# A pre-LN LRU/attention/MoE kernel on one core: three shared batches ahead of the expert tiles, one batch's gathers moved into attention, and a start of attention on two queues

## What is computed

```python
x = x + lru_block(layernorm(x))                     # layer 0: linear recurrence and an MLP
x = x + moe0(layernorm(x))                          # 8 experts of hidden 256, top 2 by softmax
x = x + attention(layernorm(x), Wq, Wk, Wv, Wo)     # layer 1: causal, 16 heads of 8
x = x + moe1(layernorm(x))                          # 8 experts of hidden 512, top 2, and a shared expert

def moe1(x):                                        # cut
    up = einsum('th,ehi->tei', xf, up_w) + up_b
    eo = einsum('tei,eih->teh', gelu(up), down_w) + down_b
    combined = einsum('teh,te->th', eo * 0.1, w)    # w: gates of the top 2
    shared = (gelu(xf @ sw_up + sb_up) @ sw_down + sb_down) * 0.1
    out = shared + combined
    return out / (max(abs(out), -1) + 1e-06)
```

## Time and profile before

| | |
|---|---|
| median of 3 runs | 972.75 us |
| lowest and highest | 966.61, 973.84 us |
| profiled execution | 970.3 us |
| its span on the chip | 968.5 us |
| mean granted TensorE clock | 0.92 |
| PE busy | 808.7 us (83%) |
| DVE busy | 613.9 us (63%) |
| ACT busy | 521.3 us (54%) |
| POOL busy | 422.9 us (44%) |

### The profile page before, as it was taken

The page is one execution under the profiler, slowest core; times in us unless marked ns, Lnnn a source line. Parts: engine busy times, 40 slices in busy tenths (PEclk is TensorE's granted clock), DMA queues, the critical chain, the costliest instruction groups (busy, mean ns, idle before and its releaser), DMA issues. The chain is left out here.

```text
span 968.5 us, 18634 instructions
## 1 busy us (share of the span) xinstructions
PE 808.7 (83%) x5585; PEld 603.0 (62%) x5585; DVE 613.9 (63%) x1402; ACT 521.3 (54%) x1092; POOL 422.9 (44%) x524
## 2 busy tenths in 40 slices
PE   2798825898559899999999999986388899999993
PEld 2566615888425556565555565546256899999762
DVE  5478653557438977877777777733811665678457
ACT  3466466665315576767767666764131466565520
POOL 2655467727578013242333332224467700273174
PEclk9899866999759999999999999995589999999997
DMA  5930013555253121212131221000012322232222
GB/s 147 366 103 1 23 46 120 158 144 139 65 171 123 39 94 39 98 33 99 43 101 65 65 97 42 26 1 0 28 44 74 106 66 76 81 114 77 77 66 65
DMA packets 82157, 80.45 MB, mean 83 GB/s; under 512 B 9858, under 2 KB 61760, under 8 KB 82112
## 3 DMA queue, kind: packets, MB, share of 16 engines
q1 hardware_dynamic: 73122, 62.68, 20.9%
q0 software_dynamic: 8192, 16.79, 5.7%
q10 hardware_dynamic: 796, 0.42, 0.2%
HBM read 41.06 MB, written 38.80 MB: 82 GB/s over the span
## 5 line engine op out<-in xcount | busy, mean ns | idle before, releaser
L1661 ACT ACTIVATE Pb<-ps,low 128x512 f32<-128x512 f32 x320 | 216.7, 689 | 134.4 <-PE ps L1760 87.6
L931 POOL DMA_INDIRECT YG<-yslots,slot x128 | 132.1, 1032 | 152.1 <-DMA yslots<-yb 82.0
L1539 DVE TENSOR_REDUCE m<-ps 128x4 f32<-128x1024 f32 x128 | 156.2, 1221 | 55.1 <-PE ps L1737 36.0
L1760 PE MATMUL ps<-Q,KZ 128*128 128x128 f32 (+3 forms) x512 | 172.1, 397 | 5.0 <-ACT Pb L1661 4.0
L390 POOL DMA_INDIRECT xslots<-XN,slot x128 | 124.7, 974 | 69.9 <-issue 37.6
L1471 POOL TENSOR_SCALAR_AFFINE_SELECT Pb<-Pb 128x512 f32<-128x512 f32 (+1 forms) x84 | 67.7, 806 | 190.0 <-ACT Pb L1661 189.3
L1760 PEld LDWEIGHTS ps<-Q,KZ 128*128 128x128 f32 x512 | 93.0, 192 | 81.8 <-ACT Pb L1661 56.1
L1313 PE MATMUL ps<-xT,wst 128*128 128x128 f32 x960 | 136.5, 280 | 7.4 <-DVE wst L1182 4.6
L1325 PE MATMUL ps<-wst,hb 128*128 128x128 f32 x960 | 134.0, 276 | 6.6 <-ACT hb L1132 6.1
L1135 ACT ACTIVATE hb<-ps,upb 128x128 f32<-128x128 f32 x320 | 91.6, 369 | 75.0 <-PE ps L1313 74.9
L1313 PEld LDWEIGHTS ps<-xT,wst 128*128 128x128 f32 x960 | 122.6, 196 | 9.1 <-DVE wst L1182 5.8
(11 more groups left out here) (258 smaller groups left out, 1240.3 us busy)
## 6 DMA issues: line engine op xcount, KB each, us to landing
xt<-xslots SPq DMA_DIRECT2D x40, 256.0 KB
yslots<-yb SPq DMA_DIRECT2D x40, 256.0 KB, 2.3
terms<-high SPq DMA_DIRECT2D x32, 256.0 KB, 2.1
Q<-terms SPq DMA_DIRECT2D x128, 48.0 KB
KZ<-terms SPq DMA_DIRECT2D x128, 48.0 KB
xslots<-YG SPq DMA_DIRECT2D x2, 2560.0 KB, 11.8
terms<-low SPq DMA_DIRECT2D x16, 256.0 KB, 2.3
X<-in_L_attn_x_dram SPq DMA_DIRECT2D x4, 512.0 KB, 5.7
```

The source lines that it names most:

```text
L931: pool.indirect_dma_start(out=s.YG[:, TB * w + j, k, :], out_offset=None, in_=s.yslots[group][:, :], in_offset=bass.IndirectOffsetOnAxis(a ...
L1539: w = dve.tensor_reduce(top[:, :, (TB + 1, 3, TB, None, 1)[u]], ps.rearrange("p (t g k) -> p g t k", t=2, g=HG), AX.XY, ALU.max)
L1661: act.activation(Pb[:, NCH * (gg % 2) + c, :], bank(4 + c % 2), ACT.Exp, bias=s.low[:, :], scale=DH ** -0.5)\
L1760: w = pe.matmul(ps[:, col:col + T - kt * P], KZ[:, HG * gg + g, kt * P:kt * P + P], Q2[gg % 2][:, kt * P:T], start=True, stop=not masked)
```

## The change

Three edits, in three places.

1. `SHARED_FIRST = 3` is set, and GD in `experts` is SHARED_FIRST: three batches of the shared expert stand ahead of layer 1's tiles and five behind them, on PE, ACT and DVE alike.
2. In layer 0's experts POOL gathers three batches instead of four. Batch 3's eight gathers stand in attention, behind `spread(0, None)` and ahead of group 1's gathers.
3. At the start of attention SP writes and reads back only the KEY part of batch 0 (three writes, 16 reads for KZ). The three QUERY writes and 16 reads for Q are issued on ACT's queue, between to_xs(1) and the first body. For the other batches nothing changes.

```diff
-LOOSE = 3
+LOOSE, SHARED_FIRST = 3, 3
...
-    GD = GROUPS[0]
+    GD = SHARED_FIRST
...
-                for b in range(FIRST[g], FIRST[g] + GROUPS[g]):
+                for b in range(FIRST[g], FIRST[g] + GROUPS[g] - (layer == 0)):
                     gather(pool, s, sums, b)
...
-            def keep(b):
-
-                for k, parts in ((KEY, (high, high, low)), (QUERY, (high, low, high))):
+            def keep(b, kinds=(KEY, QUERY)):
+
+                for k in kinds:
+                    parts = (high, low, high) if k == QUERY else (high, high, low)
                     wait_apart(sp, q["p_ready"], 2 * b + (k + 1))
...
-            def spread(b, gg, used):
+            def spread(b, gg, used, kinds=(QUERY, KEY)):
 
                 if gg == 0:
-                    for k in (KEY, QUERY):
+                    for k in kinds:
                         wait_apart(sp, kept[k], WRITES * b + WRITES)
...
-                    for k, dst in ((QUERY, Q[rows, gg, :]), (KEY, KZ[rows, HG * gg + g, :])):
+                    for k in kinds:
+                        dst = Q[rows, gg, :] if k == QUERY else KZ[rows, HG * gg + g, :]
...
-            keep(0)
+            keep(0, (KEY,))
             sp.wait_ge(s.slabs, SLABS)
             for gg in range(G):
-                spread(0, gg, None)
+                spread(0, gg, None, (KEY,))
...
             spread(0, None)
+            gather(pool, s, s.sums, FIRST[1] - 1)
             for r in range(2):
                 pool.wait_ge(s.stored[r], 16 * BODIES)
...
             to_xs(1)
+
+            act.wait_ge(q["p_ready"], 2)
+            for t, part in enumerate((high, low, high)):
+                act.dma_start(terms[QUERY][0, P * t:P * t + P, :], part[QUERY][:, :].bitcast(F32)).then_inc(kept[QUERY], 16)
+            act.wait_ge(kept[QUERY], WRITES)
+            act.wait_ge(s.slabs, SLABS)
+            heads = terms[QUERY][0:1, :, :].rearrange("b (r h) t -> h (b r) t", h=H)
+            for gg in range(G):
+                for g in range(HG):
+                    act.dma_start(Q[SLAB * g:SLAB * g + 3 * DH, gg, :].bitcast(F32), heads[G * g + gg, :, :]).then_inc(qk_in[gg], 16)
             body(0, True, False, True)
```

## The result

The changed kernel takes 959.66 us (median of 4 runs, 958.4 to 961.8) against 972.48 us for the kernel before (4 runs). The ratio is 0.9887, interval 0.9854 to 0.9919: 11 us or 1.1% less. (The ratio is not the quotient of the two medians, which would be 0.9868. Where this document gives a share in us beside an interval, it is worked out from the ratio.) A second set of runs gave 961.04 us against 970.42 us, ratio 0.9911 (0.9882 to 0.9939).

A forecast was written before the change was run, and what follows sets the result against it. PE was taken to fill most of the span, with gains only at three seams: 5.5 + 3.7 + 1.0 = 10.2 us off 970.3 gives 960.1, or 962.6 from the median; 961 was said, range 954.5 to 968.5.

The forecast's parts named there:

- the chances: Whole kernel: faster by over 1% 0.53, within 1% 0.43, slower 0.04.
- Part A: Layer 1's tail: one combine instead of two behind the last SH copy, 5.5 us less, range 5.5 down to 3.5.
- Both covers: Layer 1's experts: tiles' rows land 3.9 us before the first turn, group 1's gathers 4 us before the last combine.
- Part B: Barrier behind layer 0's experts: POOL's DRAIN ends earlier with 24 gathers, 3.7 us less; the moved gathers cost nothing in attention.
- Rival 1: Barrier behind layer 0's experts: the DRAIN waits for something other than the gathers, no gain there, 963.8 us; chance 0.12.
- Part C: Start of attention: two queues issue the first reads, scores start 1.0 us earlier; bounds +2.0 to -0.9 us.
- The other sum in the prediction: Start of attention: a second engine saves only issue time, four issues or 1.6 us, less ACT's later start.
- Rival 4: Attention: the new rhythm keeps PE's clock at 0.50 into the body, slower; 28 us longer gives 985; chance 0.04.

The follow-up runs named there:

- two_first: The changed kernel with two shared batches ahead of layer 1's tiles and six behind: 966.04 us, ratio 0.9952 to the kernel before.
- b_only: The kernel before with only batch 3's eight gathers moved into attention: 967.21 us, ratio 0.9933.
- c_reads: The kernel before with only Q's 16 reads on ACT's queue, all six writes still on SP: 971.36 us against 972.14, ratio 0.9995.
- c_only: The kernel before with only the query writes and Q's slab reads moved to ACT's queue: 969.99 us against 973.58, ratio 0.9971.
- c_writes: The kernel before with only QUERY's three writes on ACT's queue, all 32 reads still on SP: 968.89 us, ratio 0.9990.
- half_moved: The changed kernel with only four of batch 3's eight gathers moved into attention, four left ahead of the barrier: 960.94 us, ratio 0.9907 to the kernel before.
- after_again: The changed kernel run again, on the same chip as the kernel without the ACT queue edit: 961.04 us, ratio 0.9911 to the kernel before.
- a_only: The kernel before with only three shared batches ahead of layer 1's tiles: 966.29 us against 973.58, ratio 0.9927.
- a_b_again: The kernel before with the shared batch and gather edits, queues as before, run again beside the changed kernel: 963.80 us, ratio 0.9928.
- ab_reads: The changed kernel with all six writes back on SP, Q's reads still on ACT: 964.98 us, ratio 0.9932 to the kernel before.

## Why the prediction was right

- **Time.** 961 was said, 959.66 and 961.04 were measured, both within 954.5 to 968.5. The sign and the size hold. A and B carry the size; that the total comes out as close as it does with C's term in it is in part luck, as below. That the gain is over 1% holds in the first set (1.13%) and not in the second (0.89%), as close as the chances had it.
- **Part A, 5.5 us.** The tail gave 5.51 us: one combine on DVE. The gather of 2.54 us beside a combine has its like in the changed kernel, 2.56 us beside the first combine of the tail; the traces show the stretching, and not which mode DVE was in. Both covers held: the gathers' landing was 5 to 6 us early (4 forecast), and two_first shows the other cover's end, PE waiting for xt as soon as the turn could come before 32.4 us. One reading was too wide: behind SH(6) stand 8.4 us and not 10.9, and DVE was idle for only 0.86 us in them, before and after, so the combine there just fits. And the prediction put the extra work at nothing "since PE's stream does not change in length", where the clock at the first tiles took back about 1.0 us. Whether that is part A's doing is open. All seven traces with three batches ahead show the low clock there. So do b_only and c_reads, with four ahead, while c_only, c_writes and both of the kernel before do not. The first 6 us of b_only's tiles:

```profile
749.40:755.40 6.00, 3.28 (x18) 3.08 (x19) 4.03 (x10) 0.00 (x0) 4.57 (x5) 0.73 0.44 133
```

- **Part B, 3.7 us.** 3.70 us in the seam of the changed kernel, 3.7 in b_only. Rival 1 is out: half_moved moves the DRAIN with the gathers. The 10 us on POOL in attention cost nothing that the runs show: attention is 404.4 us in after_again, which has them, against 404.2 and 404.1 before. The other kernels with all eight have 405.2 to 408.9 us, but a_only, without them, has 407.7. half_moved, with half of them, times the same as the changed kernel.
- **Part C, 1.0 us.** This step failed, though its effect on the time came out with the sign forecast, which is luck. The forecast had the scores 1.0 us earlier, and 22.0 us or more behind the barrier as the sign of being wrong. They came at 23.2 to 24.3 us, 1.4 to 2.6 us later than before, in all five traces with C. Two terms were wrong. The landing of QUERY's writes was taken between 2.1 and 4.4 us and nearer the lower end, since "only three stand in line"; it was 4.42, as KZ's reads run beside them (2.7 without these, in c_writes). And the halved issue time was taken as gain; c_reads shows that it returns as landing. The other sum in the prediction, by the section of the Trainium skill that is named under c_reads (1.6 us less ACT's later start, about 2 us), was the better forecast: it gives later scores, if not late enough.
- **What C is worth.** 2.8 us in c_only, with an interval that leaves out zero (1.4 to 4.4), and 1.7 us by the ratios (2.8 by the medians) between after_again and a_b_again, unresolved by itself. Neither half alone shows a gain, but neither interval rules it out. The traces show that the stretch from the first scores to the first Exp gets shorter by 1 to 3 us with C, through an earlier and unbroken return of PE's clock, and that this makes up for the late start. Why the clock comes back after 4 to 8 us there and after 12.6 in the kernel before isn't shown, nor whether these microseconds are the gain: c_reads has a stretch shorter by 1.0 us and no gain, and attention as a whole isn't shorter on average over the traces with C. What points to the clock is its mean over the runs, which is higher with QUERY's writes on ACT in all three pairs (c_only, c_writes, after_again beside a_b_again) and not with the reads alone. The prediction expected it back "about 13 us behind the first scores, as now"; in the changed kernel it was 7.6 and 8.0. Rival 4 named the clock as a danger; it acted, in the other direction.
- **Sum of the shares.** 7.1, 6.5 and 2.8 us alone, 16.4 together, and 11 in the changed kernel. The seams account for 5.5 + 3.7. For part A the rest isn't resolved, since its interval reaches down to 5.3. For part B it is clear of the seam's 3.7 (4.6 to 8.5), and the stages of its one profile, the slowest of its six, do not show where it lies. The runs of a_only and b_only had a mean clock of 0.9232 and 0.9252 beside 0.9196 for the kernel before on that chip, so the clock is the likely source. That is argued and not shown, since a shorter wait raises the mean clock by itself.

## What to carry to other kernels

At a barrier read the instructions of the barrier itself: an engine whose last record is long past may still be what all others wait for, and work moved from ahead of it to a later idle stretch of the same engine is worth the distance to the next engine (here 3.7 us). Where two engines alternate at the end, count what stands on the second behind the last product of the first; a split that moves one unit from front to back saves one step there without changing the work, until what the front covered runs out. A second queue shortened the issuing here and not the time until all had landed, and the transfers that one queue issued beside those of the other went with a longer landing (4.4 us against 2.7). Where one program's runs spread by 11 us, take shares of 1 to 3 us from pairs of runs and seams, and look first at which execution a profile is of.

## What was not expected of the hardware

- POOL's DRAIN ended 5.8 to 6.4 us behind the last gather's record and 1.8 us behind the last scatter's; for layer 1 it was 7.9 us. The gathers' data had landed 2.5 us behind their issue in the median. What the rest is, no run tells.
- A write of 256 KB from ACT's queue beside SP's 16 reads took 3.5 to 4.4 us to land (medians by trace and tile) and up to 2.0 us to issue (c_only). Without the reads beside it (c_writes) it took 3.1 to 3.4 us to land, and the second of the three still 1.48 us to issue. From SP's queue it was 2.2 to 3.0 us, and at most 0.6 to issue.
- The granted clock between the first scores and the first Exp followed one of four courses: back after 12.6 us (the kernel before, twice); back after 6, gone at 9.7, back at 16 (four traces); back after 3.6 to 8.7 and stable (all of C, c_reads, c_writes); back only after 19.3 (ab_reads). Two traces of one program agreed within 0.5 us. Part A alone, whose edit acts over 400 us later in the program, had another course than the kernel before. Over 28 executions of one program time and mean clock moved together, 0.65 us per 0.001 of clock.
